# A graph-attention and expert-FFN kernel: GpSimd shares x's normalisation, ScalarE shares the weight and value splits, identity products run ahead, and x arrives in other parts

## The reference

```python
# N = 4096 rows of x, D = 128, 2 heads of 64, 8 experts with H = 256
xl = layernorm(x)
q, k, v = xl @ Wq, xl @ Wk, xl @ Wv                 # per head
scores = where(adj > 0, (q * 64**-0.5) @ k.T, -9e15)  # 2 x 4096 x 4096
sat = softmax(scores) @ v
out = concat(sat[:2048] @ weightr, sat[2048:] @ weightd) + bias
x = x + leaky_relu(out, 0.01)
x2 = layernorm(x)
mask = top-2 experts of x2 @ Wg + bg, as 0 or 1
x = x + sum over e of mask[e] * (gelu(x2 @ W1[e] + b1[e]) @ W2[e] + b2[e])
```

## Time and profile before

| | |
|---|---|
| Median of 3 runs | 805.73 us (805.17 to 806.05) |
| The profiled execution | 805.47 us, span 803.7 us |
| TensorE busy | 775.5 us, 96% of the span |
| ScalarE busy | 684.6 us, 85% |
| GpSimd busy | 681.6 us, 85% |
| VectorE busy | 658.4 us, 82% |

### The profile page before, as it was taken

One profiled execution on the slowest core, in us unless ns is written; L12 is line 12 of the kernel. 1 busy time (PEld: TensorE's weight loads), 2 busy tenths in 40 slices (PEclk: granted clock), 3 DMA queues, 4 the chain that ended last, 5 costly groups with the idle time before them and its releaser, 6 DMA issues.

```text
span 803.7 us, 34483 instructions
## 1 busy us (share of the span) xinstructions
PE 775.5 (96%) x13088; PEld 577.2 (72%) x13088; DVE 658.4 (82%) x1470; ACT 684.6 (85%) x1099; POOL 681.6 (85%) x673
## 2 busy tenths in 40 slices
PE   4999999999999999999999999999999999999997
PEld 2467777777777777777777777777777677777775
DVE  6887997989989898999989899998985777545554
ACT  4678887888888888888888888888988999999996
POOL 4799998999999999999998999999986767667664
PEclk9999999999999999999999999999999999999999
DMA  8633543453335334343444335334300000000000
GB/s 230 119 61 61 83 68 62 66 84 59 61 60 81 62 62 67 59 80 59 64 72 66 62 62 85 59 59 62 55 1 2 2 15 15 15 14 13 13 13 13
DMA packets 40912, 45.11 MB, mean 56 GB/s; under 512 B 22169, under 2 KB 32161, under 8 KB 40865
## 3 DMA queue, kind: packets, MB, share of 16 engines
q0 software_dynamic: 9216, 33.56, 26.4%
q1 hardware_dynamic: 31216, 10.71, 5.7%
q10 hardware_dynamic: 432, 0.20, 0.1%
HBM read 71.72 MB, written 2.10 MB: 92 GB/s over the span
## 4 chain that ended last, share of the span: by engine, by line
PE 85%; POOL 5%; DVE 4%; issue 3%; ACT 1%; DMA 1%; DVEq 0%; POOLq 0%
PE ps L1069 19%; PE ps L1090 18%; PE ps L1123 14%; PE ps L1116 9%; PE ps L1250 4%; PE ps L1251 3%; PE ps L1252 3%; PE ps L1191 3%; PE ps L1192 3%; PE ps L1193 3%; PE ps L1134 2%; POOL w_pair L366 1%; DVE pt_raw L756 1%; POOL pt_half L350 1%; PE ps L1142 1%
## 5 line engine op out<-in xcount | busy, mean ns | idle before, releaser
L734 DVE CUSTOM_DVE_ANT_0 prob<-ps,mask 128x1024 f32<-128x1024 f32 x256 | 311.1, 1221 | 28.6 <-PE ps L1069 25.0
L350 POOL TENSOR_TENSOR pt_half<-pt_raw,pt_half 128x512 f16<-128x512 f32 x252 | 301.0, 1215 | 10.5
L533 ACT ACTIVATE prob<-prob,nmax 128x1024 f32<-128x1024 f32 x256 | 292.9, 1144 | 0.2 <-DVE nmax L742 0.2
L1090 PEld LDWEIGHTS ps<-ident,prob 64*128 64x128 f32 x4096 | 154.6, 138 | 64.2 <-issue 60.2
L1069 PE MATMUL ps<-k_half,q_row 64*128 64x512 f16 x1536 | 188.1, 376 | 1.2 <-DVE k_half L684 0.8
L1090 PE MATMUL ps<-ident,prob 64*128 64x64 f32 x4096 | 180.8, 227 | 6.6 <-DVE pt_raw L756 2.2
L460 POOL TENSOR_TENSOR prob<-prob 128x512 f16<-128x512 f32 x104 | 123.7, 1194 | 56.8 <-ACT prob L611 53.9
L346 POOL TENSOR_SCALAR pt_half<-pt_raw 128x1024 f16<-128x1024 f32 x126 | 139.1, 1104 | 24.5 <-ACT pt_raw L553 9.6
L1123 PE MATMUL ps<-pt,v_sb 128*64 128x128 f32 x2048 | 126.2, 276 | 1.5 <-issue 1.5
L962 DVE SCALAR_TENSOR_TENSOR x_sb<-ps,k_half,x_sb 128x128 f32<-128x128 f32 (+1 forms) x256 | 72.1, 344 | 64.1 <-PE ps L1252 61.4
L1069 PEld LDWEIGHTS ps<-k_half,q_row 64*128 64x128 f16 x1536 | 73.7, 95 | 61.0 <-issue 6.6
(11 more groups left out here) (124 smaller groups left out, 1122.9 us busy)
## 6 DMA issues: line engine op xcount, KB each, us to landing
mask<-in_adj POOLq DMA_DIRECT2D x64, 512.0 KB, 5.4
q_row<-q_nat SPq DMA_DIRECT2D x128, 32.0 KB, 1.9
x_sb<-in_x SPq DMA_DIRECT2D x4, 512.0 KB, 7.2
out<-x_sb SPq DMA_DIRECT2D x8, 256.0 KB, 2.3
x2t_hi<-in_L_ffn_W SPq DMA_DIRECT2D x1, 1024.0 KB, 6.3
wq_sb<-in_L_gnn_Wq ACTq DMA_DIRECT2D x1, 64.0 KB, 3.2
wk_sb<-in_L_gnn_Wk ACTq DMA_DIRECT2D x1, 64.0 KB, 4.7
wv_sb<-in_L_gnn_Wv ACTq DMA_DIRECT2D x1, 64.0 KB, 6.0
```

What stands on the lines that cost most here:

```text
L350: ins = pool.tensor_tensor(pt_lo[:, q, part, :], pt_raw[:, q % 2, part, :], pt_hi[:, q, part, :], ALU.subtract)
L533: act.activation(prob[:, h, cols], prob[:, h, cols], ACT.Exp, bias=nmax[:, h:h + 1], scale=-1.0, accum_out=sums[:, j, h, p:p + 1]).then_in ...
L734: dve.tensor_tensor_reduce(out=prob[:, h, col_of(p)], in0=ps[:, 2 * (u % 2):2 * (u % 2) + 2, :].rearrange("p b c -> p (b c)"), in1=mask[:, ...
L1090: ins = pe.transpose(ps[:, bank + half, t * DH:(t + 1) * DH], prob[part, h, (p * KT + t) * P:(p * KT + t + 1) * P], ident[part, part])
```

## The change

**x's parts.** SyncE loads x in the five runs of X_RUNS (4, 4, 8, 8, 8 tiles) instead of four parts of eight. Moments and variances follow these parts; the third part's moments come in two halves, with a shift between them.

**Identity products.** TensorE multiplies the identity by itself 30 times (128x128) ahead of the first transposes, and 8 times behind the transposes of chunk 1. Nothing reads the results.

**Normalisation.** VectorE keeps its two tiles of chunk 0. Its two tiles of chunks 1 to 7 go to GpSimd (normalise_x of the gpsimd block). GpSimd's order of powers, tiles and adjacency loads is written anew.

**Value order.** Chunks are projected to v in the order 2, 3, 6, 7, 0, 1, 4, 5 (V_ORDER), so those of the split quarters 1 and 3 come first; xn_t's slots follow that order (xn_slot). For chunks 2 and 3 ScalarE also writes the high half of the values to v_first, and GpSimd only subtracts. split_values(0) and (1) both stand ahead of step(1), and split_values(0) stands ahead of load_adj(2, 0, 0).

**Weights.** The last quarter of the feed-forward weights is scaled and rounded by ScalarE, around its first three value copies; GpSimd only subtracts (low_ffn_part).

```diff
-X_PARTS = 4
-X_TILES = NT // X_PARTS
-X_CHUNKS = NC // X_PARTS
 X_RUNS = ((0, 4), (4, 8), (8, 16), (16, 24), (24, 32))
+X_PARTS = len(X_RUNS)
+WARM_UP, WARM_KEEP = 30, 8
...
+V_ORDER = (2, 3, 6, 7, 0, 1, 4, 5)
...
+        def values_of(p):
+
+            return max(V_ORDER.index(2 * p), V_ORDER.index(2 * p + 1)) + 1
...
-                part = slice(i * X_TILES, (i + 1) * X_TILES)
+                part = slice(*X_RUNS[i])
                 sp.dma_start(x_sb[:, part, :], xv[:, part, :]).then_inc(x_in[i], 16)
...
-                pool.wait_ge(v_ready, 2 * p + 2)
+                pool.wait_ge(v_ready, values_of(p))
                 if n > 0:
                     pool.wait_ge(v_lo_ready, n)
-                pool.tensor_scalar(v_pair[n][:, 0, :, :], raw, 1.0, 0.0, ALU.mult, ALU.add).then_inc(v_hi_ready, 1)
-                pool.wait_ge(v_hi_ready, n + 1)
+                    pool.tensor_scalar(v_pair[n][:, 0, :, :], raw, 1.0, 0.0, ALU.mult, ALU.add).then_inc(v_hi_ready, 1)
+                pool.wait_ge(v_hi_ready, n + 2)
...
+            def normalise_x(j):
+
+                pool.wait_ge(rstd_ready, j + 1 if j < 2 else j // 2 + 2)
+                if j >= 4:
+                    pool.wait_ge(xnt_psum, j - 3)
+                for t in range(TPC // 2):
+                    tile = j * TPC + t
+                    ins = pool.tensor_scalar(xn[:, j % 4, t, :], x_sb[:, tile, :], mv[:, tile, 0:1],
+                                             rstd[:, tile:tile + 1], ALU.subtract, ALU.mult)
+                ins.then_inc(xn_by_pool, 1)
+
+            def low_ffn_part(n):
+
+                part = slice(n * W_PART, (n + 1) * W_PART)
+                for m, (raw, pair) in enumerate(((w1_raw, w1_pair), (w2_raw, w2_pair))):
+                    pool.wait_ge(w_hi_by_act, m + 1)
+                    pool.tensor_tensor(pair[:, 1, part], raw[:, part], pair[:, 0, part],
+                                       ALU.subtract).then_inc(w_split_chain, PART_SPLITS // 2)
...
-                if early:
-                    split_values(1)
...
-            for r in range(len(X_RUNS)):
-                inverse_std_x(r)
-            for i in range(2):
-                for c in range(2):
-                    load_adj(i, i, c)
+            inverse_std_x(0)
+            inverse_std_x(1)
+            normalise_x(1)
+            inverse_std_x(2)
+            normalise_x(2)
+            normalise_x(3)
+            inverse_std_x(3)
+            load_adj(0, 0, 0)
+            load_adj(0, 0, 1)
+            normalise_x(4)
+            normalise_x(5)
+            inverse_std_x(4)
+            normalise_x(6)
+            normalise_x(7)
+            load_adj(1, 1, 0)
+            load_adj(1, 1, 1)
             pool.wait_ge(w1_in, 16)
             pool.wait_ge(w2_in, 16)
-            pool.wait_ge(xn_by_dve, NC)
             for n in range(W_PARTS - 1):
                 split_ffn_part(n)
+            low_ffn_part(W_PARTS - 1)
+            split_values(0)
             load_adj(2, 0, 0)
-            split_ffn_part(W_PARTS - 1)
             split_small()
             load_adj(2, 0, 1)
-            split_values(0)
+            split_values(1)
             step(1, 1, post=False, early=True)
...
+                if j // 2 == SPLIT_P[0]:
+                    act.activation(v_first[:, 0, j % 2 * TPC:(j % 2 + 1) * TPC, :],
+                                   ps[:, POST, :].rearrange("p (t c) -> p t c", t=TPC), ACT.Copy).then_inc(v_hi_ready, 1)
...
+            scale_weights(0, w1_raw, w1_in)
+            high_weights(0, w1_raw, w1_pair)
+            copy_v(0)
+            scale_weights(1, w2_raw, w2_in)
+            copy_v(1)
+            high_weights(1, w2_raw, w2_pair)
+            copy_v(2)
...
             row_moments(1)
             shift_x(0)
             normalise_x(0)
+            row_variances(1)
+            row_moments(2, 0, 2)
             shift_x(1)
-            normalise_x(1)
-            row_variances(1)
-            row_moments(2)
-            shift_x(2)
-            normalise_x(2)
-            normalise_x(3)
+            row_moments(2, 1, 2)
             row_variances(2)
             row_moments(3)
+            shift_x(2)
             row_variances(3)
+            row_moments(4)
             low_q(0)
+            row_variances(4)
             shift_x(3)
-            normalise_x(4)
-            normalise_x(5)
             low_k(0)
+            shift_x(4)
             low_q(1)
-            shift_x(4)
-            normalise_x(6)
-            normalise_x(7)
             low_k(1)
...
+            def multiply_ident(times):
+
+                for _ in range(times):
+                    pe.matmul(ps[:, POST, 0:P], ident[:, :], ident[:, :], start=True, stop=True)
+
             pe.wait_ge(ident_ready, 1)
+            multiply_ident(WARM_UP)
             transpose_x(0)
             transpose_x(1)
+            multiply_ident(WARM_KEEP)
```

More of the change, by code:

```diff
@@ L174, in build @@
         xn_by_dve = sem("xn_by_dve")
+        xn_by_pool = sem("xn_by_pool")
+        w_scaled_by_act = sem("w_scaled_by_act")
+        w_hi_by_act = sem("w_hi_by_act")
         xn_by_act = sem("xn_by_act")
@@ L236, in col_of, with xn_slot @@
             return slice(p * PC, (p + 1) * PC)
+        def xn_slot(j):
+            return V_ORDER.index(j)
+        def values_of(p):
+            return max(V_ORDER.index(2 * p), V_ORDER.index(2 * p + 1)) + 1
         def copies_by_dve(j, units):
@@ L356, in inverse_std_x @@
                 part = slice(*X_RUNS[r])
-                pool.wait_ge(var_ready, X_RUNS[r][0] // X_TILES + 1)
+                pool.wait_ge(var_ready, r + 1)
                 pool.tensor_tensor(rstd[:, part], ve[:, part], expo[:, part], ALU.pow).then_inc(rstd_ready, 1)
@@ L523, in _, with scale_weights, high_weights @@
                 high_k(p)
-            for j in range(V_FIRST - 1):
-                copy_v(j)
+            last_part = slice((W_PARTS - 1) * W_PART, W_PARTS * W_PART)
+            def scale_weights(m, raw, landed):
+                act.wait_ge(landed, 16)
+                act.activation(raw[:, last_part], raw[:, last_part], ACT.Copy, scale=W_UP).then_inc(w_scaled_by_act, 1)
+            def high_weights(m, raw, pair):
+                act.wait_ge(w_scaled_by_act, m + 1)
+                act.activation(pair[:, 0, last_part], raw[:, last_part], ACT.Copy).then_inc(w_hi_by_act, 1)
+            scale_weights(0, w1_raw, w1_in)
[5 more added lines that the diff above has]
+            copy_v(2)
             def exp_unit(j, u):
@@ L635, in settled, with row_moments @@
                 dve.nop(nofuse=True)
-            def row_moments(i):
+            def row_moments(i, half=0, halves=1):
+                first, end = X_RUNS[i]
+                count = (end - first) // halves
                 dve.wait_ge(x_in[i], 16)
-                for t in range(X_TILES):
-                    ins = dve.bn_stats(stats[:, t, :], x_sb[:, X_TILES * i + t, :])
-                ins.then_inc(stats_chain, 1)
+                for t in range(half * count, (half + 1) * count):
+                    ins = dve.bn_stats(stats[:, t, :], x_sb[:, first + t, :])
+                if half == halves - 1:
+                    ins.then_inc(stats_chain, 1)
             def row_variances(i):
+                first, end = X_RUNS[i]
                 dve.wait_ge(stats_chain, 2 * i + 1)
-                for t in range(X_TILES):
-                    ins = dve.bn_aggr(mv[:, X_TILES * i + t, :], stats[:, t, :])
+                for t in range(end - first):
+                    ins = dve.bn_aggr(mv[:, first + t, :], stats[:, t, :])
                 ins.then_inc(stats_chain, 1)
                 dve.wait_ge(stats_chain, 2 * i + 2)
-                part = slice(i * X_TILES, (i + 1) * X_TILES)
+                part = slice(first, end)
                 dve.tensor_scalar(ve[:, part], mv[:, part, 1], EPS, None, ALU.add).then_inc(var_ready, 1)
@@ L661, in normalise_x @@
             def normalise_x(j):
-                if j >= 4:
-                    dve.wait_ge(xnt_psum, j - 3)
                 for t in range(TPC // 2):
@@ L1003, in transpose_x @@
             def transpose_x(j):
-                pe.wait_ge(xn_by_dve, j + 1)
+                if j == 0:
+                    pe.wait_ge(xn_by_dve, 1)
+                else:
+                    pe.wait_ge(xn_by_pool, j)
                 pe.wait_ge(xn_by_act, j + 1)
@@ L1018, in project_q @@
                         pe.wait_ge(q_lo_ready, j - 1)
-                    pe.matmul(ps[:, j % 2, :], wq_sb[:, :], xn_t[:, j, :], start=True, stop=True).then_inc(q_psum, 1)
+                    pe.matmul(ps[:, j % 2, :], wq_sb[:, :], xn_t[:, xn_slot(j), :], start=True, stop=True).then_inc(q_psum, 1)
             def project_k(p):
@@ L1026, in project_k, with project_v @@
                     w = wk_sb[:, h * DH:(h + 1) * DH]
[L1027 to L1032, removed]
+                    pe.matmul(ps[0:DH, 2 + h, :], w, xn_t[:, xn_slot(2 * p), :], start=True, stop=True)
```

(16 more changed lines are left out.)

7 lines of the change are left out of this document (4 added, 3 removed).

## The result

The changed kernel takes 809.59 us (808.70 to 810.78, 6 runs) beside 805.23 (804.24 to 806.05, 6 runs) for the kernel before: ratio 1.0054, 95% interval 1.0044 to 1.0064. It is slower by 0.54%, 4.4 us. The forecast was 801.7, with 0.08 on "slower". The profiled execution took 809.48 us, its span is 807.8.

A forecast was written before the change was run, and what follows sets the result against it. TensorE bounds the kernel, held back early by the first mask_scores and late GpSimd. -2.3 (start) - 0.73 - 1.49 (GpSimd waits) + 0.5 (late half) = -4.0 from 805.47 gives 801.4, median 801.7; 8-in-10 range 800.2 to 804.9.

The forecast's parts named there:

- slower: The outcome that the changed kernel takes longer than the kernel before; chance 0.08.
- GpSimd's preparation: GpSimd before the weights: 14 normalising operations at 0.30 us make 4.2, so weights start at 22.5 instead of 25.44.
- the sum: Whole kernel: gains at the start and from GpSimd waits, less the late half's cost, make -4.0 us.
- +0.5 (late half): Tile 2's first adjacency half, issued at 43.4: VectorE waits about 2.0 us, mostly absorbed, so 0.5 charged.
- slower, by the late adjacency half alone: Rival: tile 2's half needs 12.0 us to land, giving +2.6, 808.3 us; chance 0.09, including a higher GpSimd price.
- 0.9 us a tile: GpSimd's normalising: a price above about this was counted under the slower case.
- The start: x's load and VectorE's chain: first mask_scores 2.3 us earlier, at 32.2 instead of 34.55.
- the rival in which the gaps around chunk 1 bring the lower level back: TensorE's start: first q pair keeps 3.62 us, later transposes near 17.27; within the only-half case, chance 0.27.
- TensorE's waits on GpSimd: TensorE's early idle pieces before 73.38 us: GpSimd comes 7.0 us earlier, so waits of 0.73 and 1.49 vanish.
- 3.6 us of splits: ScalarE's four weight operations and two value copies, 0.60 each, covered by its idle time from 33.19 to 44.45.

The follow-up runs named there:

- k4_const_scalars: Changed kernel with constants instead of per-row scalars in GpSimd's normalising, its halves of chunks 1 to 7 staying unnormalised: 802.08 us, ratio 0.9960.
- k5_fill: Changed kernel with 22 more identity products on TensorE ahead of the transposes of unit 4 in tile 1: 808.97 us, ratio 1.0050.
- k1_load_early: Changed kernel with load_adj(2, 0, 0) issued behind the second weight part instead of behind split_values(0): 806.91 us, ratio 1.0026.
- b2_pool_norm: Kernel before with only the normalising of chunks 1 to 7 moved to GpSimd, with its order of powers and loads: 810.14 us, ratio 1.0058.
- k9_const_loads_later: k4_const_scalars with tile 0's first two adjacency halves issued behind the last normalise_x: 802.09 us, ratio 0.9962.
- k2_dve_norm: Changed kernel with the normalising of chunks 1 to 7 back on VectorE, all else kept: 802.95 us, ratio 0.9972.
- k3_both: Changed kernel with both edits, k1_load_early's earlier load and k2_dve_norm's normalising on VectorE: 807.42 us, ratio 1.0039.
- k8_dve_norm_order: k2_dve_norm with low_q(1) ahead of shift_x(4) and the first two adjacency halves issued behind GpSimd's last power: 802.68 us, ratio 0.9967.
- k10_small_first: k8_dve_norm_order with split_values(0) and (1) moved behind both halves of tile 2 and the small weights: 800.84 us, ratio 0.9945.

## Why the prediction was wrong

**The step that failed** is the price in "GpSimd's preparation": "I take 0.30 as it is the same one-input form". The row had constants as scalars, the new operation two per-row scalars. It takes 0.78 (after), with constants 0.27 (k4_const_scalars), so the form with per-row scalars makes the difference. The upper bounds were two-input rows of other shapes, and 0.615, the one that I walked through, was still too low; the sum had no term for it either. The two tiles of chunk 1 lie ahead of the third power and delayed nothing (it was ready at 13.1, forecast 13.0). The 12 tiles of chunks 2 to 7 at 0.48 more are 5.8 us: 22.5 + 5.8 = 28.3 for the weights, 28.72 measured, and 43.4 + 5.8 = 49.2 for the half, 49.33 measured. GpSimd's walk was right, its unit price wrong.

**The term that took the error** is "+0.5 (late half)". VectorE waited 5.21 rather than 2.0, the mask took 2.58, TensorE stood 5.54, and the lower clock cost 2.5: about +8.0. Less the 2.2 of vanished waits and with +0.36 at the start that is +6.2 at attend, against 5.99 measured. I charged a delay only for itself; that a stop of TensorE can bring the lower clock, which here made it cost nearly half as much again, stood nowhere in the sum. The Trainium skill ("TensorE: Matmul & The Clock Gate", "What's actually happening") says that idle time brings the half rate back; the 0.50 from 58 to 64 us agrees, and k5_fill removes it. Not every stop did it: 3.33 us in k1_load_early did, 3.72 us in b2_pool_norm did not (1.00 throughout).

**The rival that came closest** was "slower, by the late adjacency half alone", 808.3, with the right place and the wrong reason. The load did not take 12.0 us but 5.5, as forecast; it was issued late. The 0.9 us a tile from which I let GpSimd's price decide was too high: 0.78 was enough. b2_pool_norm shows that the same price loses as much without the late half.

**The start.** x's first part landed at 3.83 (forecast 4.8). The 30 products took 9.30 us in place of 7.3, 0.31 each; that cost nothing, since GpSimd's half of chunk 1 was ready only at 11.16. The eight later ones took 1.95, 0.24 each, the price that I had used, but they were not free: ScalarE's copies of chunks 0 and 1 ended at 12.52, and the first q pair started behind the products at 13.50 and ended at 15.38 (forecast 14.1). It took 1.88, so the clock was won as forecast, and the rival in which the gaps around chunk 1 bring the lower level back did not come. But -2.3 became +0.36: VectorE's last shift stood at 24.06, where it was before (24.05), having waited 2.44 us for a power queued behind GpSimd's tiles. The price is only one half of it. With the price as forecast (k4_const_scalars) VectorE was ready at 32.6 (forecast 32.2), and the first mask_scores still came at 34.78, for q_row's issue: I had counted the adjacency loads as time on GpSimd, not what they do to SyncE's transfers. With both out of the way (k9_const_loads_later) it is 33.84, a gain of 0.7, not 2.3: there VectorE's masks were late, by the half issued later and by GpSimd's operation beside the second. No run with the normalising on GpSimd at the forecast price has q_row and the masks both early, so whether the 2.3 can be had stays open.

**TensorE's waits on GpSimd** (-0.73 and -1.49) did vanish, and in the kernels in which GpSimd is not late they stayed gone. **ScalarE's** 3.6 us of splits cost nothing to be seen: its first exponential starts at 43.03 (42.67 before), no later than the start itself is (0.36), and TensorE's wait of 0.69 us for one of its copies (at 52.03) is that of the kernel before.

**The whole, with the price right:** k2_dve_norm gave -2.3 and k4_const_scalars -3.2 where the sum said -4.0, and both contain about -1.8 that was not in the sum, the stall behind attend. That part is luck. The prediction read TensorE as busy throughout from 80 us on, from the stretch 80 to 100 alone; in the kernel before it stands still for 1.52 us ahead of 131.09. Of the forecast gain, attend shows 0.5 (72.89) to 1.0 us (72.36).

## What to carry to other kernels

Before work goes to another engine, look for that exact operand form in a trace, scalars included, and where there is none, take the price at which the change turns bad as the first thing to measure. When an engine gets later, follow the loads that it issues: a late issue can cost its whole delay at the engine that waits, and TensorE can pay for the stop a second time in clock (2.5 us here). Put a load where its buffer is already free, and long GpSimd operations where VectorE makes no mask.

## What the runs showed of the hardware that was not expected

- GpSimd's tensor_scalar on 128x128 f32 takes 0.78 us with two per-row scalars (subtract, multiply) and 0.27 with constants (multiply, add).
- VectorE's bf16 mask (128x2048) takes 0.69 us with nothing on GpSimd beside it (k3_both, at 37.49). Where a GpSimd operation is already running, the mask ends about 0.55 us after that operation does: 57.37 behind 56.82 in the changed kernel, 45.27 behind 44.71 in k8_dve_norm_order. So it takes 2.36 to 2.58 us when it begins soon after the 2.13 us subtraction does. One-input operations do it too (1.33 us at 67.08 in the changed kernel, beside a split from 66.82 to 67.86). Moved apart in k10_small_first it takes 0.72. The Trainium skill ("GPSIMD Engine Reference", "1. Specifications") states that GpSimd and VectorE share their SBUF interfaces and contend when VectorE runs in a two-port mode or reads two inputs; these rows agree that there is contention, and show that the mask waits GpSimd's operation out.
- One 32 KB q_row issue held SyncE 9.79 us with adjacency halves in flight, 1.92 with these issued later, and 5.13 in the changed kernel.
- TensorE's stop of 3.33 us in k1_load_early was followed by a granted clock of 0.54 (64 to 66 us), the stop of 3.72 us in b2_pool_norm by 1.00.
- The 1.5 us "issue" stall of TensorE, present in some instruction sequences and absent in others, is as large as most edits here. With 22 products more it came as 0.8, with 38 in the kernel before it moved from tile 5 to about 95 us. Its cause is open, so a gain of 1.5 us on this kernel should not be put down to an edit before the waits are read.
